# A chunked gated delta-rule layer with an FP6 feed-forward: in-chunk solve weights stored transposed, and twelve and eight DMA completion slots for ten and six

## The reference

```python
def step(S, inp):                       # 16 heads, S is 64 x 64
    k_t, q_t, v_t, beta_t, a_t = inp
    S = S * a_t
    kv_mem = einsum('bhd,bhde->bhe', k_t, S)
    delta = (v_t - kv_mem) * beta_t
    S = S + k_t[..., :, None] * delta[..., None, :]
    y_t = einsum('bhd,bhde->bhe', q_t, S)
x = x + layernorm(rmsnorm(y) * silu(gate) @ Wo.T + bo)     # attention part of layernorm(x)
x = x + layernorm(quant_fp6(layernorm(x)) @ quant_fp6(W).T + bias)
```

## Time and profile before

| | |
|---|---|
| median of 3 runs | 6966.59 us (6966.46 to 6967.97) |
| the profiled execution | 6967.01 us; its span on the slowest core 6965.5 us |
| spans of the 8 cores | 6915.2 to 6965.5 us |
| mean granted TensorE clock | 0.586 to 0.589 of full speed |
| busy share of the span | PE 39%, PEld 23%, DVE 39%, ACT 15%, POOL 10% |
| DMA | 269.90 MB, 39 GB/s over the span |

### The profile page before, as it was taken

How to read it: one execution, slowest core, us unless ns; L and a number is a source line. 1 busy time by engine, 2 the same in 40 slices (tenths; PEclk the granted TensorE clock), 3 DMA queues, 4 the chain that set the end, 5 groups by cost and what they waited for, 6 DMA issues and landing times.

```text
span 6965.5 us, 73275 instructions; the slowest of 8 cores (6915.2 to 6965.5 us)
## 1 busy us (share of the span) xinstructions
PE 2714.1 (39%) x22136; PEld 1583.3 (23%) x22136; DVE 2700.5 (39%) x6430; ACT 1055.6 (15%) x2275; POOL 677.3 (10%) x1048
## 2 busy tenths in 40 slices
PE   2214334444413434444422515445431515444441
PEld 1101122323301112323310203223310103233220
DVE  2241134444462124444454114444445014444446
ACT  1111111111111111111111111111111211111111
POOL 1100111101000111101000011111000011111000
PEclk9999655555556655555556855555555855555555
DMA  4412121212102112212201212112201212122210
GB/s 84 72 39 51 21 39 35 46 31 43 34 12 60 36 31 38 40 34 42 45 14 44 51 20 49 34 31 47 43 20 35 59 14 46 31 38 43 41 32 21
DMA packets 427092, 269.90 MB, mean 39 GB/s; under 512 B 235396, under 2 KB 414086, under 8 KB 426710
## 3 DMA queue, kind: packets, MB, share of 16 engines
q1 hardware_dynamic: 382934, 212.72, 13.9%
q0 software_dynamic: 43776, 52.49, 4.9%
HBM read 246.06 MB, written 27.44 MB: 39 GB/s over the span
## 4 chain that ended last, share of the span: by engine, by line
DVE 30%; DMA 28%; PE 19%; issue 14%; ACT 6%; DVEq 2%; POOL 1%; SPq 0%; ACTq 0%; POOLq 0%
DMA wrep<-wd 13%; DVE ptm L885 6%; DVE u L889 6%; PE ppr L602 3%; DVE rr L635 3%; DMA wdst<-sc 2%; PE ptr L894 2%; PE psu L907 2%; DMA prow<-pd 2%; DVE rr L946 2%; PE pys L920 1%; DVEq L1205 1%; PE ptr L627 1%; DVE st L496 1%; PE pys L848 1%
## 5 line engine op out<-in xcount | busy, mean ns | idle before, releaser
L894 PE MATMUL ptr<-idf,u 128*16 128x128 f32 x1024 | 258.8, 406 | 1369.4 <-DVE u L889 1251.8
L811 DVE TENSOR_TENSOR wrep<-wrep,bb 128x2048 f32<-128x2048 f32 x128 | 293.4, 2292 | 1072.2 <-DMA wrep<-wd 1072.2
L889 DVE TENSOR_TENSOR u<-u,ptm 128x120 f32<-128x120 f32 (+14 forms) x1920 | 448.7, 234 | 206.7 <-DVE ptm L885 9.9
L885 DVE TENSOR_TENSOR ptm<-wrep,u 128x120 f32<-128x120 f32 (+14 forms) x1920 | 447.7, 233 | 193.7 <-DVE u L889 8.0
L843 PE MATMUL pkv<-kc,s 64*64 64x16 f32 x4096 | 479.8, 265 | 45.2 <-DVE kc L819 45.2
L843 PEld LDWEIGHTS pkv<-kc,s 64*64 64x64 f32 x4096 | 454.5, 220 | 74.0 <-issue 69.9
L848 PE MATMUL pys<-qc,s 64*64 64x16 f32 x4096 | 460.8, 264 | 21.3 <-ACT ys L927 21.3
L635 DVE RECIPROCAL rr<-rr 2x1024 f32<-2x1024 f32 x32 | 209.3, 6540 | 663.4 <-ACT rr L631 663.4
L848 PEld LDWEIGHTS pys<-qc,s 64*64 64x64 f32 x4096 | 450.8, 222 | 30.1 <-issue 30.1
L894 PEld LDWEIGHTS ptr<-idf,u 128*16 128x16 f32 x1024 | 99.9, 112 | 1516.2 <-issue 1476.3
L602 PE MATMUL ppr<-lt,wrhs 128*128 128x512 bf16 x1280 | 346.2, 419 | 215.5 <-DMA wrhs<-wtk 31.1
(11 more groups left out here) (207 smaller groups left out, 3984.5 us busy)
## 6 DMA issues: line engine op xcount, KB each, us to landing
wrep<-wd SPq DMA_DIRECT2D x256, 512.0 KB, 5.2
sx<-x SPq DMA_DIRECT2D x4, 2048.0 KB, 8.0
ao<-pd SPq DMA_DIRECT2D x32, 256.0 KB, 5.3
out<-sx SPq DMA_DIRECT2D x4, 2048.0 KB, 6.6
wld<-Wf SPq DMA_DIRECT2D x8, 512.0 KB, 5.3
wrhs<-wtq POOLq DMA_DIRECT2D x16, 256.0 KB, 3.8
wrhs<-wtq SPq DMA_DIRECT2D x16, 256.0 KB, 2.9
wrhs<-wtk SPq DMA_DIRECT2D x16, 256.0 KB, 3.0
```

What stands on the lines that cost most here:

```text
L811: VE(lambda e, wv=wv, bb3=bb3: e.tensor_tensor(wv, wv, bb3, ALU.mult), [f"wrep{cp}", "bb"], [f"wrep{cp}"], tag="wrepscale")
L885: VE(lambda e, wsl=wsl, ub=ub, ptv=ptv: e.tensor_tensor(ptv, wsl, ub, ALU.mult), ["u", f"wrep{cp}"], ["ptm"], tag="slv_p")
L889: VE(lambda e, usl=usl, ptv=ptv: e.tensor_tensor(usl, usl, ptv, ALU.add), ["u", "ptm"], ["u"], tag="slv_u")
L894: TE(lambda e, hp=hp, hpi=hpi: e.transpose(p_tr[0:16, hpi * 128:(hpi + 1) * 128], s_u[:, hp * C:(hp + 1) * C], s_idf[:]), ["u", "idf", "ptr"],
```

## The change

The weights are laid out with the target token outside and the source token inside, where the source was outside: the decay difference is taken the other way round, the mask is the other triangle (which the kernel holds already as `ntril`, so the constant `ntriu` and its load go), L811 repeats `bb` over the source token, and L885 reads a column of the block. And the two DMA queues get two more completion slots each.

```diff
@@ -36,7 +36,7 @@
 ENGINES = ("sync", "tensor", "vector", "scalar", "gpsimd")
 
 
-DMA_SLOTS = {"sync": 10, "gpsimd": 6}
+DMA_SLOTS = {"sync": 12, "gpsimd": 8}
 
 
 class Plan:
...
@@ -296,7 +291,6 @@
     dma("sync", s_idb[:], d_idb, [], ["idb"])
     dma("sync", s_ntril[:], d_ntril, [], ["ntril"])
     dma("sync", s_ttri[:], d_ttri, [], ["ttri"])
-    dma("sync", s_ntriu[:], d_ntriu, [], ["ntriu"])
     dma("sync", s_esel[:], d_esel, [], ["esel"])
     dma("sync", s_e2t[:], d_e2t, [], ["e2t"])
     dma("sync", s_mka[:], d_mska, [], ["mka"])
...
@@ -703,18 +697,25 @@
         dumpd = d_qk if incl else d_wd
         dkey = ("dqk" if incl else "dwd") + str(par)
         pcol = s_ppt[:, w * H:(w + 1) * H].unsqueeze(2).broadcast_to((128, H, 16))
-        GE(lambda e, pcol=pcol: e.tensor_tensor(
-            s_mt[:].rearrange("p (h i) -> p h i", h=H),
-            s_prow[:].rearrange("p (h i) -> p h i", h=H), pcol,
-            ALU.subtract),
-           ["prow", "ppt"], ["mt"])
+        if incl:
+            GE(lambda e, pcol=pcol: e.tensor_tensor(
+                s_mt[:].rearrange("p (h i) -> p h i", h=H),
+                s_prow[:].rearrange("p (h i) -> p h i", h=H), pcol,
+                ALU.subtract),
+               ["prow", "ppt"], ["mt"])
+        else:
+            GE(lambda e, pcol=pcol: e.tensor_tensor(
+                s_mt[:].rearrange("p (h i) -> p h i", h=H), pcol,
+                s_prow[:].rearrange("p (h i) -> p h i", h=H),
+                ALU.subtract),
+               ["prow", "ppt"], ["mt"])
         GE(lambda e: e.tensor_scalar_min(s_mt[:], s_mt[:], 0.0), ["mt"], ["mt"])
         SE(lambda e: e.activation(out=s_mt[:], in_=s_mt[:], func=AF.Exp),
            ["mt"], ["mt"])
         GE(lambda e: e.tensor_tensor(s_wdst[:], s_wdst[:], s_mt[:], ALU.mult),
            ["mt", "wdst"], ["wdst"])
-        mk = s_ttri if incl else s_ntriu
-        mkk = "ttri" if incl else "ntriu"
+        mk = s_ttri if incl else s_ntril
+        mkk = "ttri" if incl else "ntril"
         GE(lambda e, mk=mk: e.tensor_tensor(s_wdst[:], s_wdst[:], mk[:],
                                             ALU.mult),
            ["wdst", mkk], ["wdst"])
...
@@ -805,9 +806,9 @@
                                cp * 2048:(cp + 1) * 2048],
                 srcw, [f"dwd{par}"], [f"wrep{cp}"], tag="wrepload")
         wv = s_wrep[:, cp * 2048:(cp + 1) * 2048].rearrange(
-            "p (h i j) -> p h i j", h=NP, i=C)
+            "p (h j i) -> p h j i", h=NP, j=C)
         bb3 = win_slice(s_bb, w % 4)[:, :, k * C:(k + 1) * C] \
-            .unsqueeze(2).broadcast_to((128, NP, C, C))
+            .unsqueeze(3).broadcast_to((128, NP, C, C))
         VE(lambda e, wv=wv, bb3=bb3: e.tensor_tensor(wv, wv, bb3, ALU.mult),
            [f"wrep{cp}", "bb"], [f"wrep{cp}"], tag="wrepscale")
 
...
@@ -879,7 +880,7 @@
             ucol = uv[:, :, m]
             width = C - 1 - m
             wsl = s_wrep[:, cp * 2048:(cp + 1) * 2048].rearrange(
-                "p (h i j) -> p h i j", h=NP, i=C)[:, :, m, m + 1:]
+                "p (h j i) -> p h j i", h=NP, j=C)[:, :, m + 1:, m]
             ub = ucol.unsqueeze(2).broadcast_to((128, NP, width))
             ptv = s_ptm[:].rearrange("p (h t) -> p h t", h=NP)[:, :, 0:width]
             VE(lambda e, wsl=wsl, ub=ub, ptv=ptv: e.tensor_tensor(
```

More of the change, by code:

```diff
@@ L111, in build_consts @@
         np.broadcast_to(triincl[None, :, None, :], (NCH, C, H, C)).reshape(128, H * C))
-    ntriu = -(j[None, :] > j[:, None]).astype(np.float32)
-    c["ntriu"] = np.ascontiguousarray(
-        np.broadcast_to(ntriu[None, :, None, :], (NCH, C, H, C)).reshape(128, H * C))
     e = np.zeros((128, 2), dtype=np.float32)
@@ L148, in build_program @@
     d_ttri = inp("triincl", (128, H * C))
-    d_ntriu = inp("ntriu", (128, H * C))
     d_esel = inp("esel2", (128, 2))
@@ L199, in build_program @@
     s_ttri = sbuf("ttri", (128, H * C))
-    s_ntriu = sbuf("sntriu", (128, H * C))
     s_esel = sbuf("esel", (128, 2))
@@ L1264 @@
         triincl=consts["triincl"],
-        ntriu=consts["ntriu"],
         esel2=consts["esel2"],
```

## The result

The changed kernel takes 7184.3 us (median of 8 runs, 7180.1 to 7190.9) against 6967.3 us of before on the same chips: ratio 1.0314, 95% interval 1.0303 to 1.0326, so 217 us or 3.1% slower. The forecast was 7247. The profiled execution took 7186.9 us, its span 7185.3 us.

The account below looks back on a forecast made before the run. A chain of waits was taken to bound the kernel, no engine busy above 39%. 6967.0 + 174 (`prow` wait) + 127 (column read) + 9 (L920 wait) - 30 (weight stream) = 7247 us, range 7110 to 7320.

Parts of the forecast that it names:

- the free column: Rival: L885's column read of the transposed weights costs nothing; 7144 us, chance 16%.
- L885's wide form: Sign: the widest products of the solve at L885 would take near 400 ns in place of 280.
- the period that ends with chunk 3's start: Sign: in 12 windows, the time up to chunk 3's start would be near 40 us, the other periods near 25.6.
- 2a, the `prow` wait: Chunk 4's `wrep` load on SP waits for the last `prow` load: 14.5 us in 12 windows, 174 us.
- 1, the transposed weights: L885 in the solve reads a column, one more element time per element: 127 us over 128 chunks.
- 2b, L920: SP's wait for the `qkb` products moves to chunk 3 and newly appears at chunk 2 in four windows: +9 us.
- 2c, the first `ao` load: A window's first `ao` load waits for the end of chunk 7's solve, some 5 us later, but covered: cost 0.
- 2d, the weight stream: GpSimd's weight loads for the two output products wait less with eight slots: -30 us.
- two more element times: Rival: L885's column read costs 254 us in place of 127; 7350 us, chance 4%.
- a covered `prow` wait: Rival: the last `prow` load lands before chunk 2's solve ends, so chunk 4's load isn't delayed; 7073 us, chance 6%.
- Deeper queues win: Rival: `prow` waits covered and column read free, so the freed weight stream decides; 6946 us, faster, chance 2%.
- The collision named as a sign of being wrong: Sign against the forecast: a delayed chunk 3 lets other loads collide with the dump of `wd`; no size given.

Follow-up runs that it names:

- `prow` under a second name: Changed kernel with what the `prow` loads read given a name of its own, so slots no longer wait for those loads: 6998.5 us, ratio 1.0067.
- the step rows: Kernel before with VectorE products and copies added behind its end, operands packed or read at wider word steps; timed per instruction, the execution's time not used.

## Why the prediction was right

The direction, both causes of the loss and the one gain were as told; each sits in its own run. The sizes were less good. The forecast with both costs had a range of its own, 7205 to 7320, and 7184 lies below it. It lies in the part of the full range (7110 to 7320) that was added for the free column, and the column isn't free. The price of the column read was held fixed at its upper bound in that range, and that is the term that took the time out of it. It is partly luck that the total is only 63 us off: the column was 59 us too dear and the delay some 25 us too cheap. Of the signs, L885's wide form was to be near 400 ns and took 348; the period that ends with chunk 3's start was to be near 40 us and took 498.7/12 = 41.6; L811 and L889 kept their times. Term by term:

*2a, the `prow` wait: right, 174 too small.* 202.1 us with slots alone, and 203.4 - 5.5 = 198 in the changed kernel, over the layout alone. The chain from the first extract to the load was 48.6 us over the 12 windows and eight cores (49.3 in the window shown) where I had 48.3. What I took off it was too large: from the first extract to the end of chunk 2's solve it went from 29.8 to 31.8 us, and not to 34.0. The two longer solves gave 1.05 of that (layout alone: 30.85), since the price of the column was half of mine. The wait for L920 gave 0.9 (slots alone: 30.7) and not 2.3. In the four first windows of a block it is new and lengthens this stretch by 1.96. In the eight others it only moves, out of one period of the same stretch into the next, and adds 0.4. So the delay was 48.6 - 31.8 = 17 us for 14.5.

*1, the transposed weights: right, but the size was half.* 68 us for 127. The step that failed is the price of one more element time, read from the 8-element form. That form isn't slow for the reason I gave: a step costs nothing at 8 elements (167 and 167 ns), and it took 174 after as it took 175 before. So it was no evidence of any price, nor of the rule about lines that I set beside it, and the right direction of this term was partly luck. Why it is 8 ns above its line stays open. Long forms pay 0.74 ns an element; at 120 the form of the kernel pays 0.6 ((348 - 277)/120). The other row, the copy L575, held a truth that I passed over: its excess was small.

*2b, L920: right.* 16 waits; with slots alone the periods of chunks 1 and 2 together grow by 12.0 us, where I had 9.

*2c, the first `ao` load: right, no cost.* The cover was there, 32 us a window. From a window to the next +5.5 us in all, and the layout alone gives +7.6.

*2d, the weight stream: right.* -38 us in its own run, for -30. I had counted the waits alone, and they fell by 28.5. Most of the rest is TensorE's clock. These are stretches of the attention output product of the second block (L1000) in the kernel before (`--windows`: us, busy time of PE, PEld, DVE, ACT and POOL, then the granted clock, the DMA share and GB/s):

```profile
3540.30:3543.00 2.70, 2.70 (x7) 1.05 (x8) 0.00 (x0) 0.00 (x0) 0.00 (x0) 0.50 0.00 0
3543.30:3548.00 4.70, 4.13 (x20) 1.73 (x19) 0.00 (x0) 0.00 (x0) 1.07 (x2) 1.00 0.40 109
...
3560.60:3565.00 4.40, 2.56 (x6) 0.50 (x4) 1.38 (x3) 0.59 (x1) 0.77 (x2) 0.50 0.22 58
```

At a granted clock of 0.50 (1.2 GHz) L1000 starts a product every 0.43 us, at 1.00 (2.4 GHz) every 0.215. The clock was at 0.50 behind a stretch in which TensorE was mostly idle (3535.5 to 3540, busy 1.1 of 4.5 us), rose at 3543, and was at 0.50 again from 3560.6, after an idle time of 2.79 us for a load of `wrhs`. From the kernel before to that with eight slots on GpSimd, the matmuls of L1000 and L1058 that lasted 0.63 us or more, where others last 0.38, fell from 99 to 70 of 508 on a core, and the busy time of the two lines from 221.5 to 213.0 us. So a wait for a weight slice cost more here than its own length.

*A term I had left out.* The 68 other periods grew by 23.4 us, with the layout alone by 36.8, and with slots alone they shrank by 12.7. So about -13 us belongs to the delay itself. The traces say where it comes from. In the kernel before, 634 of the 30720 products and additions of the solves on the eight cores took over 20 ns more than the median of their form, the longest 0.96 us more. Each of the 634 overlaps one of the four instructions of `_score_maskdump` on GpSimd (L706, L711, L714, L718), and no product or addition that overlaps none of them took so long. Of those that started while a TENSOR_TENSOR of GpSimd was running, 418 of 419 did; 609 others overlap GpSimd's work and took their usual time. Two of the 634, at 3176 and 3178 us; without GpSimd they take 0.19 and 0.17:

```profile
3176.34 0.56 DVE L885 TENSOR_TENSOR ptm<-wrep,u 128x32 f32<-128x32 f32 x1
3178.72 0.59 DVE L889 TENSOR_TENSOR u<-u,ptm 128x8 f32<-128x8 f32 x1
```

```profile
3176.23 0.62 POOL L706 TENSOR_TENSOR mt<-prow,ppt 128x256 f32<-128x256 f32 x1 [1.97 <-DMA prow<-pd]
3178.56 0.72 POOL L714 TENSOR_TENSOR wdst<-wdst,mt 128x256 f32<-128x256 f32 x1 [0.66 <-ACT mt L712]
```

They lie in the solves of chunks 3 and 6 of the windows with pieces. With the delay, chunk 3's solve starts only after GpSimd is through, at 3283.7 against 3273.5 in the window shown above. The extra time in chunk 3's solves, as the mean of a core, beside the change of the period from chunk 3 to chunk 4:

| kernel | extra time in chunk 3's solves, us | that period against before, us |
|---|---|---|
| before | 10.2 | |
| slots alone | 0.0 | -10.7 |
| layout alone | 14.8 | +12.7 |
| changed, `prow` under a second name | 16.1 | +14.1 |
| changed | 0.0 | -2.1 |

Where the layout is the new one, 8.2 to 8.7 us of the second column are its own, as in the periods of chunks 1, 2, 5 and 6; with that the two columns agree within 0.5 us. This is read from the traces of five kernels; no run moved GpSimd's instructions alone.

The terms as measured, in the changed kernel over the layout alone: 198 (chunk 3) + 14 (L920) - 13 (GpSimd) - 40 (blocks) - 1 (the rest) + 68 (layout) = 226 us, as in the mean span. With the column read at 68 and the delay at 17.0 the forecast's sum would have been 6967 + 204 + 68 + 9 - 30 = 7218.

Of the rivals, the free column is refuted by the layout alone (+67), two more element times by the step rows, and a covered `prow` wait by the trace and by the second name. "Deeper queues win" is true of GpSimd's queue, which feeds half of the weight stream, and only there. The collision named as a sign of being wrong does take place, since the delayed load now runs beside the dumps of `wd`, but it costs nothing that shows: the halves land in 4.95 and 4.94 us, against 5.12 and 5.45 before. The Trainium skill, "SBUF — State Buffer", Specifications (two hits on a 16-byte line for full rate), agrees with these rows: step 2, two words to a line, took 283 ns as packed did, step 4 took 366. One result a cycle, which the Trainium skill, "VectorE: DVE Perf Modes", Mode 1× (REGULAR) — the baseline, gives for this mode with odd strides too, doesn't agree with them: 1.78 ns an element at step 4 against 1.04 packed.

## What to carry to other kernels

When a planner reuses completion slots, count back through the queue's program order before you change the number: what the slot's former user touched decides what the new one waits for, and one shared read-only name cost 2.5% here. A slot needs only its own former DMA; let data dependences carry the rest, and name halves of a buffer apart when they are loaded apart. Before moving a transpose out of a producer and into the reader's step, price the reader at its own length: words 16 bytes or more apart cost VectorE here 0.6 to 0.74 ns an element more from 120 elements on and nothing at 8, and on a serial solve all of it is paid. Look, too, at what GpSimd computes while VectorE is on the critical path: in the kernel before, solve steps that ran beside it lost 32 us a core.

## What wasn't expected of the hardware

The price of a stepped operand on VectorE is a threshold, not a slope: 283 ns at 8 bytes, 366 at 16, 354 at 64, for 120 elements, and 372 with three such operands; 12 bytes wasn't tried. An element takes 1.7 element times and not 2, and the extra is gone at 8 elements (167 and 167 ns) and nearly so at 16 (179 against 175).

The solve's products and additions took up to 1 us more when they started while a TENSOR_TENSOR of GpSimd was running (418 of 419 in the kernel before), though the two work on different tiles.
